# Last pair of the Mamba block: a new front with two convolution tiles on TensorE, the gate half later, and another order inside the loop over its states

## The chip, the cores and the metric

One core of one Trainium2 chip runs the whole program. It has five engines with a queue each: TensorE (PE) multiplies, VectorE (DVE), ScalarE (ACT) and GpSimd (POOL) work elementwise, and SyncE (SP) issues the DMAs. Each queue runs in its own order, and an instruction starts when the semaphores that it waits for have the counts asked for. The metric is the device time of one execution in microseconds, the median of the runs.

## The reference

```python
x = x + xattn(ctx, layernorm(x))          # 16 heads, 64 latents per sequence, 1024+64 keys
x = x + mamba(layernorm(x))               # below
x = x + ffn(layernorm(x))                 # 8 experts, each gathers tokens by a list and scatters back

# mamba, for x of (8, 64, 256): 512 inner channels, 16 states, 4 taps
xn = layernorm(x) * norm_w + norm_b
xc, z = split(xn @ W_in)
xc = silu(sum(x_pad[:, k:k + 64] * conv_w[:, k] for k in range(4)) + conv_b)
dbc = xc @ x_proj_w                       # 33 rows: one for dt, 16 of B, 16 of C
dt = softplus(dbc[0] * dt_w + dt_b)
h[n, t] = exp(dt * A[n]) * h[n, t-1] + dt * B[n, t] * xc      # for each of 16 states n
y = (sum_n h[n, t] * C[n, t] + xc * D) * silu(z)
out = y @ W_out + x
```

## The kernel before

**Stages.** The 8 sequences of 64 tokens form four pairs of 128 tokens (t = 0 to 3). The cross attention runs as 64 steps of a head pair, 8 for each sequence. The Mamba work of pairs 0 to 2 is woven into the attention steps: for each pair and state a unit `u = 16 t + n` is opened on POOL (`open_unit`, L630: work = dtx times B), scanned on DVE (`scan_unit`, L974), multiplied with C on POOL (`close_unit`, or late `times_c`, L752), and summed. For the last units TensorE adds the products up in PSUM bank `WB` (`sum_unit`, L1967). Eight units are left when the attention ends: u8, u9 and u10 of the drain, and `left[0]` to `left[4]`.

**The last pair (t = 3, INLINE)** can only start when the attention of its two sequences is done. Its front, one step behind the other: statistics and normalised tokens `xn`; two transposes to `xn_t`; `in_proj(0)` (the x half of W_in, four tiles of 128 channels) and `in_proj(1)` (the z half, the gate) on TensorE (L1795); four taps of the convolution over four tiles on DVE (L1163, L1166, 16 instructions); silu on ACT (`xc`, L1520); `x_proj` (L1802); `dbc` copied out (L1526); row 0 of `dbc` spread over the partitions by `spread` (L1813), from it the softplus on DVE and ACT (`dt_abs`, L1529 to L1531), then `dts_l` and `dtx_l` on DVE (L1194, L1197). Rows of B 0 to 3 come to `b_all` by TensorE and ACT (semaphore `m_b`), the others by three DMAs; rows of C come four at a time by `spread_out`.

**The loop over its 16 states**, in each engine's own order: POOL `drive` (L777, dtx_l times B, up to four ahead), ACT four exponentials into PSUM (L1558, bank `DB[n % 2]`), DVE the scan `state` (L1208) and `read` (L1218, state times C), TensorE adds `read` up in PSUM (`sum_states`, L2019, one matmul over 512 columns, which the trace shows as two records). Beside it the queues carry other work: the last units; `side_job` (transposes of `pick`, the one-hot token lists of the experts, L2024, and ACT's copy L1540, four states later; the transposed weights `coef_t`; two matmuls with b2); eight `slot_weight` (four matmuls each, L2062); `w_out` of pair 2 (L1808) and its residual; and the first `gather` matmuls.

**The way to the experts.** The normalised tokens of each pair are split in `f_hi` and `f_lo`. `gather(g, k, t)` is two matmuls over 512 columns (L2054) for expert group g, channel half k and pair t: 16 calls in all. Their four banks are copied to `xg_t` (L1577), then come W1 (L2147), Gelu (L1587, `hid`), W2 (L2157) and the way back to the tokens (L2134).

**What sets the order.** Every queue is written out by hand; there is no planner. Buffers: three `work` (a unit waits for the sum of the unit three before it), four `bc` rows loaded by DMA (each after the sum of the unit four before it), four `drive`, three `state`, two `read`. All of the last pair's queues are in the four blocks after `all_steps(body, drain)`.

## Time and profile before

| | us |
|---|---|
| median of 3 runs | 768.75 (768.65 to 770.01) |
| profiled execution, its time | 769.03 |
| its span, first to last instruction | 767.3 |
| PE, DVE, ACT, POOL busy in the span | 735.2, 493.9, 432.5, 399.7 |
| mean granted TensorE clock | 0.984 |

The attention's last matmul into the residual ends at 612.4 us and the first expert's second layer starts at 695.41 us; everything the change touches lies between these two times. "Busy" of PE counts pipelined matmuls with modelled ends, so it is read together with the granted clock and with the idle times in brackets, which name the engine and line that ended them.

### The profile page before, as it was taken

To read this page: it belongs to the slowest core of one execution; us is meant where nothing else is said; L and a number is where in the kernel's file an instruction comes from. 1 tells how busy PE (TensorE), PEld (TensorE's weight loads), DVE (VectorE), ACT (ScalarE), POOL (GpSimd) and SP (SyncE) were. 2 spreads that over 40 slices of the span, in tenths; PEclk is the share of its full clock that TensorE was granted. 3 is DMA by queue.
4 is the path that set the end of the run, shared out by engine and by line. 5 is a ranking of instruction groups with operands and counts; after the bars stand their busy time and mean duration, and the time that the engine had idled before them with its cause. 6 is when DMAs were issued, how large, how long until landed. Compare 5 with 4: busy or idle time off the path is not lost.

```text
span 767.3 us, 14591 instructions
## 1 busy us (share of the span) xinstructions
PE 735.2 (96%) x5539; PEld 681.3 (89%) x5539; DVE 493.9 (64%) x1061; ACT 432.5 (56%) x1135; POOL 399.7 (52%) x355
## 2 busy tenths in 40 slices
PE   8999999999999999999999999999999886999995
PEld 8889999999998999999989999999999663578885
DVE  7574574556574667858777778686798886840102
ACT  2546456546355766566578666666656553734331
POOL 6515315302610389658838986587397978730000
PEclk9999999999999999999999999999999995999999
DMA  8742100011001200310211022000100107703800
GB/s 308 243 138 60 63 25 2 1 62 25 2 5 59 53 16 1 95 34 16 65 32 34 15 68 55 15 15 1 33 15 21 28 22 234 254 1 129 285 26 30
DMA packets 51418, 49.62 MB, mean 65 GB/s; under 512 B 19524, under 2 KB 46352, under 8 KB 50320
## 3 DMA queue, kind: packets, MB, share of 16 engines
q1 hardware_dynamic: 51344, 48.64, 20.9%
q8 instruction: 46, 0.75, 0.4%
q14 instruction: 28, 0.23, 0.1%
HBM read 44.10 MB, written 4.52 MB: 63 GB/s over the span
## 4 chain that ended last, share of the span: by engine, by line
PE 69%; POOL 14%; issue 8%; DVE 5%; ACT 3%; DMA 1%; POOLq 0%; DVEq 0%
PE psum L1701 18%; PE psum L1736 17%; PE psum L1717 5%; PE psum L2157 4%; PE psum L2147 4%; POOL work L630 3%; PE psum L1670 3%; POOL work L637 2%; POOL y_sum L643 2%; PE psum L1767 2%; PE psum L1677 2%; PE psum L1795 2%; POOL drive L777 1%; PE psum L1611 1%; PE psum L1777 1%
## 5 line engine op out<-in xcount | busy, mean ns | idle before, releaser
L1347 ACT ACTIVATE pt_hi<-psum 128x512 fp32r<-128x512 f32 (+1 forms) x192 | 87.2, 489 | 179.9 <-PE psum L1717 122.0
L1736 PE MATMUL psum<-kvn_hi,pt_hi 128*128 128x256 f32 x512 | 150.1, 293 | 0.0
L1736 PE MATMUL psum<-kvn_hi,pt_lo 128*128 128x256 f32 x512 | 144.3, 282 | 0.0
L1736 PE MATMUL psum<-kvn_lo,pt_hi 128*128 128x256 f32 x512 | 144.2, 282 | 0.0
L1043 DVE TENSOR_REDUCE rowmax<-psum 128x1 f32<-128x728 f32 x64 | 58.6, 915 | 79.2 <-PE psum L1701 79.2
L1736 PEld LDWEIGHTS psum<-kvn_lo,pt_hi 128*128 128x128 f32 x512 | 97.4, 190 | 0.2
L1736 PEld LDWEIGHTS psum<-kvn_hi,pt_hi 128*128 128x128 f32 x512 | 97.1, 190 | 0.2
L1736 PEld LDWEIGHTS psum<-kvn_hi,pt_lo 128*128 128x128 f32 x512 | 97.1, 190 | 0.0
L1701 PE MATMUL psum<-kvt_hi,qk_hi 128*128 128x364 f32 (+1 forms) x384 | 90.5, 344 | 0.0
L896 DVE TENSOR_TENSOR pt_lo<-psum,pt_hi 128x512 fp32r<-128x512 f32 x128 | 82.0, 682 | 8.2 <-ACT pt_hi L1347 8.2
L637 POOL TENSOR_TENSOR work<-work,bc 128x512 f32<-128x512 f32 x40 | 54.3, 1357 | 58.6 <-DVE work L974 58.6
L1701 PE MATMUL psum<-kvt_hi,qk_lo 128*128 128x364 f32 (+1 forms) x384 | 84.5, 328 | 0.0
L1701 PE MATMUL psum<-kvt_lo,qk_hi 128*128 128x364 f32 (+1 forms) x384 | 84.5, 329 | 0.0
L974 DVE TENSOR_TENSOR_SCAN work<-dec,work 128x512 f32<-128x512 f32 x48 | 73.6, 1536 | 6.4 <-POOL work L630 6.1
L575 POOL TENSOR_SCALAR cvar<-cmv 128x8 f32<-128x8 f32 x8 | 1.9, 232 | 131.5 <-DVE cmv L835 131.1
L630 POOL TENSOR_TENSOR work<-dtx,bc 128x512 f32<-128x512 f32 x48 | 65.2, 1361 | 8.4 <-DMA bc<-dbc_keep 6.6
L1717 PE MATMUL psum<-ident,prob 128*128 128x128 f32 x512 | 66.5, 273 | 1.4 <-DVE pt_hi L893 0.8
L1701 PEld LDWEIGHTS psum<-kvt_lo,qk_hi 128*128 128x128 f32 x384 | 66.6, 188 | 0.0
L1701 PEld LDWEIGHTS psum<-kvt_hi,qk_lo 128*128 128x128 f32 x384 | 66.5, 188 | 0.0
L1701 PEld LDWEIGHTS psum<-kvt_hi,qk_hi 128*128 128x128 f32 x384 | 63.2, 189 | 2.2 <-issue 0.4
L1423 ACT ACTIVATE dec<-dts,a_neg 128x126 f32<-128x126 f32 x192 | 60.7, 394 | 5.9 <-DVE work L974 5.3
L1467 ACT ACTIVATE prob<-psum,nbias 128x728 f32<-128x728 f32 x64 | 55.7, 870 | 13.4 <-DVE nbias L1045 11.1
(251 smaller groups left out, 1576.5 us busy)
## 6 DMA issues: line engine op xcount, KB each, us to landing
w<-in_L_ffn_W_dram SPq DMA_DIRECT2D x16, 1024.0 KB, 8.2
ctx_nat<-in_ctx_dram SPq DMA_DIRECT2D x8, 1024.0 KB, 5.1
bc<-dbc_keep SPq DMA_DIRECT2D x48, 128.0 KB, 4.5
q_cur<-q_keep SPq DMA_DIRECT2D x14, 128.0 KB, 3.0
q_keep<-q_t SPq DMA_DIRECT2D x1, 1536.0 KB, 6.0
wq_sb<-in_L_xattn_Wq_dram SPq DMA_DIRECT2D x1, 1024.0 KB, 10.6
wk_nat<-in_L_xattn_Wkv_dram SPq DMA_DIRECT2D x1, 1024.0 KB, 12.7
wv<-in_L_xattn_Wkv_dram SPq DMA_DIRECT2D x1, 1024.0 KB, 14.7
```

The lines of the kernel that those rows point to most:

```text
L630: pool.tensor_tensor(work[u % WORKS][:], dtx[:], bc[u % ROWS][:, 0:1, :].to_broadcast((P, DT, P)), ALU.mult).then_inc(v_drv, 1)
L637: link(pool.tensor_tensor(work[u % WORKS][:], work[u % WORKS][:], bc[u % ROWS][:, 1:2, :].to_broadcast((P, DT, P)), ALU.mult))
L896: dve.tensor_tensor(pt_lo[u][:, t0:t1, :], where.rearrange("p (t m) -> p t m", m=P), pt_hi[u][:, t0:t1, :].bitcast(F32), ALU.subtract).the ...
L974: dve.tensor_tensor_scan(work[u % WORKS][:].rearrange(flat), dec[u % 2][:].rearrange(flat), work[u % WORKS][:].rearrange(flat), 0.0, ALU.m ...
L1043: dve.tensor_reduce(rowmax[slot][:, hp, 0:1], LG_A, XY, ALU.max)
L1347: act.activation(pt_hi[u][:, t0:t1, :], where[:, 0:(t1 - t0) * P].rearrange("p (t m) -> p t m", m=P), ACT.Copy)\
L1423: last = act.activation(seqs(dec[u % 2][:])[:, d, :, 1:], seqs(dts[:])[:, d, :, 1:], ACT.Exp, scale=a_neg[:, d, n:n + 1])
L1467: act.activation(prob[hp % 2][:, 0:2 * CUT].rearrange("p (a n) -> p a n", n=CUT), LG_A, ACT.Exp, bias=nbias[slot][:, hp:hp + 1], scale=SCA ...
L1701: last = pe.matmul(psum[:, n, 0:x1_ - x0], w, x_[slot][:, k, x0:x1_], start=first, stop=final)
L1717: last = pe.transpose(TP[n][:, j * P:(j + 1) * P], prob[hp % 2][:, (4 * n + j) * P:(4 * n + j + 1) * P], ident[:])
L1736: pe.matmul(PV, w[u][:, j, :], x_[slot][:, j, :], start=(j == 0 and w is pt_hi and x_ is kvn_hi), stop=False)
L2147: last = pe.matmul(psum[:, f % 4, 0:P], w1[i][:, k, f * P:(f + 1) * P], xg_t[:, k, RING * q + i, :], start=(k == 0), stop=(k == CK - 1))
```

## The change

It touches only the last pair, from the statistics to the first expert, and the places of other work in the same queues:

- **Convolution.** Tiles 2 and 3 (`PE_TILES`) leave DVE. ACT builds eight diagonal matrices `tap_w` (identity times one tap of a tile) after the drain; TensorE projects tiles 2 and 3 first, into bank `JB`; ACT copies them into the padded `xpad`; TensorE adds four products `tap_w` times shifted `xpad` for each tile; ACT's silu reads PSUM with the bias. DVE keeps 8 of its 16 tap instructions.
- **Gate half.** `in_proj(1)` moves behind the softplus input `v_dl`. ACT copies it and takes its silu after the loop.
- **Softplus.** Row 0 is spread twice; ACT takes Abs straight from PSUM with scale and bias, beside DVE's linear form.
- **Fillers.** The ten matmuls ahead of `x_proj` (`FILL_XC`) are gone.
- **Left units.** Of `left[0..4]`, DVE and POOL do two ahead of the loop in place of three, and three inside it (behind states 1, 3, 5 on DVE).
- **Slot weights and gathers.** The eight `slot_weight` move from states 12 to 15 to states 1 to 8, one for each; four gathers of pairs 0 and 1 sit behind states 12 and 13 in place of two calls at the end; `coef_slot` is reduced inside the loop.
- **Tokens for the experts.** POOL makes `f_hi` as well (ACT did), for pair 0 ahead of the loop, for pair 1 behind drive 11, for pair 2 behind the last drive. The last pair's `f_hi` comes from x directly on DVE.
- **Expert head.** The gathered banks are `GB = ((0, 1), (4, 7))`; ACT copies half k = 0 and DVE half k = 1. The Gelu table is loaded ahead of the gathers' end.
- `token_norm` of the last pair: the two small variance instructions go from POOL to DVE.

```diff
@@ POOL @@
-            for u in left[1:3]:
-                open_unit(u)
+            link(pool.memset(fhalf[:], -0.5))
...
+            open_unit(left[1])
             pool.wait_ge(r_pos, 2)
...
+            row_scale(0, 2)
+            pool.wait_ge(v_xt, INLINE + 2)
+            row_parts(0)
             times_c(left[0])
...
-            times_c(left[1])
-            open_unit(left[3])
-            times_c(left[2])
-            open_unit(left[4])
             pool.wait_ge(v_dtx, INLINE + 1)
             pool.wait_ge(m_b, 2)
-            for n in range(2):
+            drive_open(0)
+            drive_open(1)
+            open_unit(left[2])
+            drive_open(2)
+            times_c(left[1])
...
@@ DVE @@
-            scan_unit(left[0])
+            first_pick(1)
             dve.wait_ge(v_xz, INLINE + 1)
             dve.wait_ge(v_dts, INLINE)
+            own = DT - len(PE_TILES)
             for k in reversed(range(TAPS)):
                 late = TAPS - 1 - k
-                for d in range(DT):
+                for d in range(own):
...
@@ ACT @@
+                for k in range(TAPS):
+                    act.activation(tap_w[:, n, k, :], ident[:], ACT.Copy, scale=convw[:, d, k:k + 1])
...
+            act.wait_ge(m_xp, 1)
+            act.activation(xpad[:, PE_TILES[0]:, :, TAPS - 1:],
+                           psum[:, JB, 0:C].rearrange("p (d s l) -> p d s l", s=BP, l=L), ACT.Copy).then_inc(v_pad, 1)
...
+            for n, d in enumerate(PE_TILES):
+                act.wait_ge(m_cv, len(PE_TILES))
+                act.activation(xc[:, d, :], psum[:, JB, C + n * P:C + (n + 1) * P], ACT.Silu,
+                               bias=dvec[:, 0, d:d + 1]).then_inc(v_xc, 1)
...
+            act.wait_ge(m_dt0, 2)
+            for d in range(DT):
+                last = act.activation(dt_abs[:, d, :], psum[:, CB[1], 0:P], ACT.Abs, scale=dvec[:, 1, d:d + 1],
+                                      bias=dvec[:, 2, d:d + 1])
...
@@ PE @@
-            in_proj(0, psum[:, YB, :]).then_inc(v_xz, 1)
-            in_proj(1, psum[:, ZB, :]).then_inc(v_xz, 1)
+            in_proj(0, psum[:, JB, :], PE_TILES).then_inc(m_xp, 1)
+            in_proj(0, psum[:, YB, :], range(DT - len(PE_TILES))).then_inc(v_xz, 1)
...
-            sum_unit(u10)
-            fill(FILL_XC)
+            pe.wait_ge(v_pad, INLINE + 1)
+            for n, d in enumerate(PE_TILES):
+                for k in range(TAPS):
+                    last = pe.matmul(psum[:, JB, C + n * P:C + (n + 1) * P], tap_w[:, n, k, :], xpad[:, d, :, k:k + L],
+                                     start=(k == 0), stop=(k == TAPS - 1))
+                last.then_inc(m_cv, 1)
...
             pe.wait_ge(v_dl, INLINE + 1)
+            in_proj(1, psum[:, ZB, :]).then_inc(v_xz, 1)
+            sum_unit(u10)
...
-            sum_unit(left[1])
+            pe.wait_ge(m_dta, 1)
             spread_out(1)
-            sum_unit(left[2])
...
+                if 1 <= n <= E:
+                    last = slot_weight(n - 1)
+                    if n == E:
                         last.then_inc(f_cs, 1)
```

POOL's queue from the last `tshift` of the last pair to the first drives, before (work are the units' tiles, drive those of the loop):

```order
L656 TENSOR_SCALAR tshift<-tshift 128x1
L630 TENSOR_TENSOR work<-dtx,bc 128x512
L752 TENSOR_TENSOR work<-work,bc 128x512 x2
L630 TENSOR_TENSOR work<-dtx,bc 128x512 x2
L765 TENSOR_SCALAR coef_hl<-coef 128x32
L766 TENSOR_TENSOR coef_hl<-coef,coef_hl 128x32
L752 TENSOR_TENSOR work<-work,bc 128x512
L770 TENSOR_TENSOR y_skip<-xc,dvec 128x512
L752 TENSOR_TENSOR work<-work,bc 128x512
L630 TENSOR_TENSOR work<-dtx,bc 128x512
L752 TENSOR_TENSOR work<-work,bc 128x512
L630 TENSOR_TENSOR work<-dtx,bc 128x512
```

The first two drives come right behind these rows. The same stretch of POOL's queue after the change:

```order
L635 TENSOR_TENSOR work<-dtx,bc 128x512
L762 TENSOR_TENSOR work<-work,bc 128x512 x2
L772 MEMSET fhalf 128x4
L635 TENSOR_TENSOR work<-dtx,bc 128x512
L792 TENSOR_SCALAR coef_hl<-coef 128x32
L793 TENSOR_TENSOR coef_hl<-coef,coef_hl 128x32
L777 TENSOR_SCALAR fvar<-fmv 128x2
L778 TENSOR_TENSOR frstd<-fvar,fhalf 128x2
L782 TENSOR_SCALAR xn<-x,fmv,frstd 128x256
L785 TENSOR_SCALAR f_hi<-xn 128x256
L787 TENSOR_TENSOR f_lo<-xn,f_hi 128x256
L762 TENSOR_TENSOR work<-work,bc 128x512
```

Then come y_skip and the first two drives: two unit products and three unit openings have moved behind drives, and five instructions for the tokens of pair 0 have come in.

TensorE's queue behind the transposes of `xn` of the last pair, up to the spreads of `dbc`, before:

```order
L1795 MATMUL psum<-xn_t,win 128x128 x16
L1987 MATMUL psum<-ident,b_rows 128x64
L1967 MATMUL psum<-work,ident 128x512 x2
L1973 MATMUL psum<-ident 128x128 x10
L1802 MATMUL psum<-xc,wxp 33x128 x4
```

and after:

```order
L1859 MATMUL psum<-xn_t,win 128x128 x8
L2051 MATMUL psum<-ident,b_rows 128x64
L2031 MATMUL psum<-work,ident 128x512
L2056 MATMUL psum<-xpad,tap_w 128x128 x8
L1866 MATMUL psum<-xc,wxp 33x128 x4
L1877 MATMUL psum<-dbc,ident 128x128 x6
L1859 MATMUL psum<-xn_t,win 128x128 x8
```

Eight projections, one unit sum and the ten fillers have left the place ahead of `x_proj`, and eight tap matmuls stand there.

TensorE's queue inside the loop, from state 1 to state 3, after (read is summed by L2089, pick turned by L2094, the slot weights are L2132; before, the rows L2132 were absent here and stood, eight at a time, behind the sums of states 12 to 15):

```order
L2031 MATMUL psum<-work,ident 128x512
L2094 MATMUL psum<-ident,pick 128x128 x4
L2132 MATMUL psum<-coef_hl,pick 128x2 x4
L2089 MATMUL psum<-read,ident 128x512
L2094 MATMUL psum<-ident,pick 128x128 x4
L2132 MATMUL psum<-coef_hl,pick 128x2 x4
L2089 MATMUL psum<-read,ident 128x512
L2031 MATMUL psum<-work,ident 128x512
```

Each state from 1 to 8 now carries four small matmuls more, and every second one a unit's sum.

## Rows read from the trace of the kernel before

**Rows 1.** By stretch: length; busy PE, PEld, DVE, ACT, POOL; granted clock; DMA
```profile
627.00:640.50 13.50, 10.57 (x33) 5.85 (x34) 7.34 (x9) 8.59 (x26) 13.04 (x11) 0.63 0.15 43
640.50:647.00 6.50, 1.82 (x3) 0.25 (x1) 6.44 (x6) 2.47 (x8) 4.06 (x3) 0.50 1.00 302
647.00:651.00 4.00, 3.91 (x5) 1.85 (x6) 3.41 (x5) 1.24 (x4) 4.00 (x4) 0.50 1.06 390
651.00:667.00 16.00, 15.38 (x69) 9.15 (x69) 14.20 (x17) 11.94 (x35) 12.94 (x12) 1.00 0.95 331
667.00:680.80 13.80, 13.58 (x58) 7.30 (x56) 9.36 (x13) 7.54 (x22) 6.80 (x12) 1.00 0.00 1
```

**Rows 2.** Timeline of POOL: start, us, operation, idle before it and who ended it
```profile
617.04 1.27 POOL L630 TENSOR_TENSOR work<-dtx,bc 128x512 f32<-128x512 f32 x1
618.26 3.41 POOL L752 TENSOR_TENSOR work<-work,bc 128x512 f32<-128x512 f32 x2
622.98 1.27 POOL L630 TENSOR_TENSOR work<-dtx,bc 128x512 f32<-128x512 f32 x1 [1.30 <-PE psum L1967]
627.32 1.31 POOL L630 TENSOR_TENSOR work<-dtx,bc 128x512 f32<-128x512 f32 x1 [3.07 <-DMA bc<-dbc_keep]
...
639.19 2.48 POOL L777 TENSOR_TENSOR drive<-dtx_l,b_all 128x512 f32<-128x512 f32 x2
```

**Rows 3.** Groups by shape on POOL: count, busy us, mean ns, idle before
```profile
L803 POOL TENSOR_SCALAR dec<-x,fmv,frstd 128x256 f32<-128x256 f32 x3 | 3.7, 1227 | 0.7 <-POOL frstd L800 0.7
...
L806 POOL TENSOR_TENSOR f_lo<-dec,f_hi 128x256 fp32r<-128x256 f32 x3 | 2.2, 727 | 6.6 <-ACT f_hi L1595 6.6
```

**Rows 4.** Timeline of DVE, front, first state, last tokens
```profile
618.41 2.21 DVE L974 TENSOR_TENSOR_SCAN work<-dec,work 128x512 f32<-128x512 f32 x1 [0.89 <-POOL work L630]
...
621.80 3.13 DVE L1166 SCALAR_TENSOR_TENSOR conv<-psum,convw,conv 128x126 f32<-128x126 f32 x12
...
640.56 1.22 DVE L1208 TENSOR_TENSOR_SCAN state<-psum,drive 128x512 f32<-128x512 f32 x1 [5.00 <-POOL drive L777]
...
686.89 0.43 DVE L1253 TENSOR_TENSOR f_lo<-dec,f_hi 128x256 fp32r<-128x256 f32 x1 [0.49 <-ACT f_hi L1595]
```

**Rows 5.** Timeline of ACT, front of the last pair
```profile
625.29 1.28 ACT L1521 ACT_TABLE_LOAD   x1
...
626.95 0.27 ACT L1526 ACTIVATE dbc<-psum 33x128 f32<-33x128 f32 x1
...
630.52 0.63 ACT L1531 ACTIVATE dt_abs<-dt_abs 128x512 f32<-128x512 f32 x1
```

**Rows 6.** Timeline of PE, front and one state of the loop
```profile
617.73 3.84 PE L1795 MATMUL psum<-xn_t,win 128*128 128x128 f32 x32 [0.55 <-ACT xn_t L1511]
...
629.22 1.15 PE L1813 MATMUL psum<-dbc,ident 33*128 33x128 f32 x8 [0.57 <-DVE conv L1188]
...
652.97 1.02 PE L2019 MATMUL psum<-read,ident 128*128 128x512 f32 x2
653.83 0.60 PE L2024 MATMUL psum<-ident,pick 128*128 128x128 f32 x4
654.27 1.02 PE L2019 MATMUL psum<-read,ident 128*128 128x512 f32 x2
```

**Rows 7.** Chain that ended last, in order of time: start, us, what
```profile
678.56 0.79 PE psum L2062 x8
...
682.12 1.73 PE psum L1808 x8
683.85 5.14 PE psum L2054 x22
...
689.01 2.07 ACT xg_t L1577 x4
...
691.09 1.28 ACT L1582
...
695.41 3.72 PE psum L2157 x16
```

230 lines of the change are left out of this document (136 added, 94 removed).

## The prediction

> **What bounds the kernel now.** I read the busy times by stretch first, then the timelines of the engines that wait, then the chain. Three regimes follow one another. From 627 to 640.5 POOL is busy 13.04 of 13.50 us while DVE has 7.34 [rows 1]: POOL's queue of unit products and openings holds back the first drive, which starts at 639.19 [rows 2], and DVE's first state scan waits 5.00 us for it, to 640.56 [rows 4]. Up to 651 the queue of DVE and POOL goes on. TensorE has 1.82 of 6.50 us between 640.5 and 647, at a granted clock of 0.50 (1.2 GHz). From 651 on the clock is full and TensorE is busy 15.38 of 16.00 and 13.58 of 13.80 us [rows 1]: it bounds the rest of the loop, and in the chain its rows follow one another without a gap to w_out at 682.12 [rows 7]. The third regime is the way to the first second layer at 695.41: gathers, then 2.07 us of copies and 1.28 us of table load on ACT, both bare in the chain [rows 7]. Time won in the front is therefore worth only what TensorE's own list after 645 leaves of it, and time won in the third regime counts in full.
>
> **Front.** DVE's taps lose half of their instructions: the 12 with an addition took 3.13 us [rows 4], six take about 1.6. The x half is 16 matmuls in two halves; the two halves together with the gate were 3.84 us at 617.73, 0.24 a matmul (32 records, two to a matmul) [rows 6]. So tiles 2 and 3 are projected after 0.96 us and tiles 0 and 1 after 1.92, at 619.7, about as late as before for DVE, which then ends at 622. The eight tap matmuls cost 8 x 0.24 = 1.9 us. They stand behind the sum of u9, whose product POOL ends about 620.8 (1.27 + 2 x 1.2 to 1.7 us from 617.04 [rows 2]), so they run from 621.7 to 623.6, and silu ends near 624.3. Before, the table load behind silu began at 625.29 [rows 5]; it now begins about 1.0 us earlier. The row of dbc comes at 625.9 in place of 626.95. The diagonal matrices are ACT work while ACT waits for the norm, priced at nothing. If that cover were gone they would cost 8 instructions of some 0.3 us, since four silus of the same shape at about 0.25 ended just ahead of 625.29. The ten fillers stood where TensorE waited for silu anyway: nothing.
>
> Behind dbc the softplus needs Abs, Exp and Ln. The last took 0.63 [rows 5]; Abs in four pieces is between 0.63 and 1.3, I take 1.0. It starts from the second spread, without DVE's linear form between them. dts_l and dtx_l are then there at 630.5 to 631. The other input of a drive is b_all, which now lies behind the gate half (8 x 0.24 = 1.9), the sum of u10 (0.9) and four spreads (1.15 at 629.22, eight records [rows 6]) from v_dl at 627.8: 631.7, and ACT's copy makes it 632.3.
>
> **POOL** decides, as before. Its queue from 617.04 to the first drive: two openings and four products (6 x 1.27 = 7.6), y_skip 1.27, coef_hl 1.6, and for pair 0 the scale 0.8, the normalised rows 1.23, f_hi and f_lo. f_lo took 0.73 [rows 3]; f_hi on POOL has no row, between 0.4 and 1.23, and I take 0.5, since it reads one operand where f_lo reads two. Sum 13.7, less one product counted in the 620.8 (left[1]'s now lies behind drive 2), 12.4. Collisions come on top: the two products at 618.26 took 3.41 beside DVE's scan of 2.21 [rows 2, 4], against 2 x 1.27 and a free scan's 1.22, so about 0.9 each time. Four such meetings are 3.6. First drive at 617.04 + 12.4 + 3.6 = 633.0, and the first scan at about 635.3, some 5.2 us earlier than 640.56. What vanishes is 1.30 us of waiting for a sum and 3.07 us for a row's DMA [rows 2], and two products and three openings that went behind drives.
>
> **Loop.** Those units now sit between drives 1 and 8. POOL (some 14 items at 1.24 to 1.7 us each up to drive 8) and DVE (three unit scans) therefore keep the first states slow, and state 0's lead shrinks already there. The sum of state 1 starts near 644.5. From there TensorE's list to the last sum is: 15 state sums and 4 unit sums at 0.86 (652.97 to 653.83) to 0.98, I take 0.89, 16.9; eight turnings at 0.44 (653.83 to 654.27) 3.5 [rows 6]; eight slot weights at 0.79 for two [rows 7] 3.2; two spreads of four 2.2; w_out 1.73; four gather calls at 2 x 5.14/22 = 0.47 [rows 7] 1.9; coef_t 0.44, b2 two at 0.89, 1.8. Together 31.7 us. At half clock the sums double; before, the clock was back at full by 651 [rows 1]. I take 650, three sums at half, 2.6 us. The last sum ends at 644.5 + 31.7 + 2.6 = 678.8, the gate product and its two semaphores add 0.9 to 1.0, so w_out starts at **679.8** against 682.12: 2.3 us of the front's 5.2. The rest is given back because TensorE, once full, was the bound already, and slot weights and gathers that move to the front of its list don't become less. The waits ahead of the slot weights (f_hl, m_b) were met long before. The wait ahead of the first gathers is for the second b2 copy, and behind it the sum of state 13 and DVE's last reads are queued; the copy takes some 0.6 beside a sum of 0.89, so it costs 0 to 0.3, taken as 0 since the copy was asked for a state earlier. The zs silu now comes after the exponentials, with a table load of 1.28 [rows 5]: the last exponentials end near 675.5, so it is done about 677.9, one microsecond ahead of need. If the loop came out faster than I say, this would be late next.
>
> **Head of the experts.** Before, 695.41 - 682.12 = 13.3 us [rows 7]. Now: w_out 1.73; 12 gather calls (14 before, behind w_out) at 0.47, 5.6; the first layers of two experts, 16 matmuls at 0.24, 3.8; the last Gelu 0.4 with its semaphores. 11.6 us, **1.7** less: two calls, and ACT's copies and table load no longer in the path, since group 0 is copied by ACT and DVE while group 1 is gathered. The cover of the last pair's normalisation shrinks from ten calls to eight, 3.7 us; before, f_lo came at 687.3, 3.5 us after w_out ended [rows 4, 7]. DVE's own f_hi takes out ACT's round trip, so it keeps inside. If not, it costs a few tenths.
>
> The trace has a table load of 1.28 us with the next ACT instruction 0.01 us behind it [rows 5, 7]. The Trainium skill, page ScalarE: Activation LUTs, section What ACT_TABLE_LOAD costs, puts a drain of about 1.38 us on top, 2.66 in all. By it the head would give 3.1 and the sum 763.3; the row speaks against it.
>
> **Sum.** 2.3 + 1.7 = 4.0 off the profiled 769.03, 765.0; the median of the runs lies 0.3 below the profiled run, so **764.7**. About 0.2% (1.5 us) is what a measurement can tell from no change.
>
> **Rivals.** *B, POOL jams.* Five token instructions and two openings stand ahead of drive 0 beside DVE's picks and scans. If every one collides as at 618.26, the first drive is 2.2 us later, 635.2, and nearly all of it reaches w_out: 766.7. For: 3.41 and 2.21 [rows 2, 4]; against: the reads of the taps come from PSUM. The Trainium skill, page SBUF — State Buffer, section 🔬 SBUF: two separate sides, makes it an exclusive lock: a GpSimd instruction and a DVE instruction with two SBUF inputs never share, the later one waits whole. These rows fit it.
>
> *C, the clock is back early.* With less idle time for TensorE than before its clock may not fall, or return by 647. Of the 2.6 us above about 1.2 come back, then DVE and POOL bound: 763.5.
>
> *D, the clock falls early.* The fillers and two sums leave the place ahead of x_proj. If TensorE is at 0.5 from 627 (before, the mean was 0.63 over 627 to 640.5 [rows 1]), gate half, sum and spreads take 3.9 more, the first drive waits for b_all until about 636, and some half of that is swallowed later: 766.3.
>
> *E, the front doesn't come.* Silu's products on TensorE wait for ACT's copy of the projections and for the sum of u9. If x_proj is no earlier and POOL's drives come one microsecond earlier only, sum 1 is at 648.5, w_out at 682, and the head's 1.7 us alone is left, less the loss of a wait at state 12: 767.7.
>
> *A, slower.* TensorE's list is now heavier in states 1 to 8. If the clock stays at 0.5 beyond 650, each microsecond costs about 0.4 (half of the time is sums and spreads that double). The gain is gone when full clock comes at 660; at 664.5 the time is 4.0 - 0.4 x 14.5 = -1.8: 770.5. Against it: at 651 the clock rose with a busy TensorE for four microseconds [rows 1].
>
> **Chances.** Forecast (763.8 to 765.9) 0.50; B 0.12; C 0.12; D 0.10; E 0.10; A 0.06. Faster by over 0.2%: 0.50 + 0.12 + 0.12 + 0.10 = 0.84; within 0.2% E, 0.10; slower A, 0.06. The range leaves out E and A and the tail of C: 762.8 to 767.5. It covers f_hi's bounds (0.1 less, 0.7 more) and the wait at state 12 (0.3).
>
> **What would show it.** In the timeline of POOL the first drive at 632.5 to 634 (B: over 635, with products of 2 us and more); in ACT's, dbc at 625.9 (E: 626.5 or later); in the stretches, the clock at full by 650 and TensorE busy 96% from there to 678; state 15 scanned near 674.5, w_out at 679.8, the second layer at 691.4. I am wrong on the loop if w_out is over 681 while the first scan is at 635.5 and the clock as said; wrong on the head if w_out to the second layer is over 12.3 us.

## The result and the profile after

| | before | changed |
|---|---|---|
| median, us | 769.04 (768.65 to 770.01, 5 runs) | 764.62 (763.97 to 765.90, 5 runs) |
| ratio | | 0.9943, 95% interval 0.9932 to 0.9955 |
| profiled execution: time, span | 769.03, 767.3 | 764.62, 762.8 |

Three differences between the two profiled spans make up the 4.5 us, read from the timelines of PE. From the start to the last pair's w_out: 681.96 before, 678.55 after, 3.41 less (0.40 of it was there when the attention ended, 612.42 and 612.02, which the change doesn't touch). From w_out to the first second layer: 13.45 before, 11.76 after, 1.69 less. From there to the end of the span: 71.89 before, 72.49 after, 0.60 more.

By stretch, the changed kernel (length; busy PE, PEld, DVE, ACT, POOL; granted clock; DMA share; GB/s), to set beside [rows 1]:

```profile
622.00:626.00 4.00, 2.77 (x24) 2.31 (x23) 3.27 (x5) 2.45 (x5) 3.64 (x6) 1.00 0.14 35
626.00:630.00 4.00, 3.66 (x20) 3.46 (x19) 2.25 (x5) 3.65 (x10) 3.83 (x5) 0.57 0.00 0
630.00:634.00 4.00, 4.00 (x22) 2.36 (x21) 2.54 (x2) 2.18 (x7) 1.73 (x2) 1.00 0.09 18
...
642.00:645.00 3.00, 1.91 (x3) 0.88 (x4) 2.17 (x3) 3.00 (x11) 2.81 (x3) 0.50 0.92 301
645.00:648.00 3.00, 3.00 (x12) 1.77 (x11) 3.00 (x4) 0.53 (x2) 3.00 (x3) 0.67 1.04 370
648.00:651.00 3.00, 3.00 (x14) 1.74 (x13) 2.85 (x5) 2.91 (x10) 3.00 (x4) 1.00 1.05 395
651.00:667.00 16.00, 16.00 (x87) 11.33 (x86) 13.53 (x17) 10.32 (x30) 15.83 (x14) 1.00 0.94 328
```

TensorE is busy without a gap from 645 to the last state's sum at 677.8, and the clock is full again at about 647.0, 4 us earlier than before the change (651). From 626 to 630 the granted clock was 0.57 although TensorE was busy 3.66 of 4.00 us. PE's timeline has the gate half in that stretch, and later the first sums, which wait for DVE's reads:

```profile
626.93 3.48 PE L1859 MATMUL psum<-xn_t,win 128*128 128x128 f32 x16 [0.34 <-DVE conv L1224]
...
639.68 2.07 PE L2089 MATMUL psum<-read,ident 128*128 128x512 f32 x2 [4.14 <-DVE read L1253]
643.09 2.07 PE L2089 MATMUL psum<-read,ident 128*128 128x512 f32 x2 [1.33 <-DVE read L1253]
644.96 1.92 PE L2031 MATMUL psum<-work,ident 128*128 128x512 f32 x2
```

The gate half (8 matmuls, 16 records) took 3.48 us; before the change it was half of the 3.84 us in [rows 6]. POOL's timeline, to set beside [rows 2]:

```profile
617.47 3.48 POOL L762 TENSOR_TENSOR work<-work,bc 128x512 f32<-128x512 f32 x2
...
629.37 1.48 POOL L800 TENSOR_TENSOR y_skip<-xc,dvec 128x512 f32<-128x512 f32 x1
633.12 2.48 POOL L807 TENSOR_TENSOR drive<-dtx_l,b_all 128x512 f32<-128x512 f32 x2 [2.27 <-ACT b_all L1596]
```

POOL's queue was through at 630.85; it then waited 2.27 us for ACT's copy of the B rows. The first scan on DVE answers to [rows 4]:

```profile
634.49 1.22 DVE L1243 TENSOR_TENSOR_SCAN state<-psum,drive 128x512 f32<-128x512 f32 x1 [1.95 <-POOL drive L807]
```

So the first scan came 6.07 us earlier (640.56 to 634.49). From it to the sum of state 2, 13.15 us where it had been 12.41 (652.97 less 640.56): 0.74 given back. From that sum to w_out, 30.91 where it had been 28.99: 1.92 given back. The second number is TensorE's list. Behind the sum of state 2 stand three unit sums more than before (3 x 0.86 = 2.6) and two gather calls more (0.9), and the slot weights take 0.8 less (7 x 0.34 in place of 8 x 0.40): 2.7 together. PE's busy time in this stretch grew by 2.0 only, from 28.15 to 30.13 us, and its idle time hardly changed (0.84 before; 0.78 after, which is all the wait for the gate product ahead of w_out). The other 0.7 us are my reading, not a measurement: before the change a sum twice started 0.75 us behind a turning (659.64 to 660.39, 661.35 to 662.10) where turnings otherwise take 0.44, because it waited for DVE's read, and the modelled ends count that wait as busy.

This also corrects a reading in the prediction. Before the change, the chain was not TensorE's alone from 651 on. It ran over POOL's drives and DVE up to 662, and over TensorE mainly from there:

```profile
649.97 7.38 POOL drive L777 x6
...
661.38 0.67 DVE read L1218
...
671.61 1.13 PE psum L2019 x2
```

TensorE, POOL and DVE were close to level in that loop; only with the change does TensorE run it without a gap.

**What moved the first drive.** Before the change its two inputs were there at 633.35 (dtx_l) and 631.64 (b_all), and POOL's queue reached it at 639.19. After it they are there at 631.40 and 632.99, and the queue is through at 630.85. By these times nearly all of the 6.07 us is the unit work that went behind the drives, with its waits of 1.30 and 3.07 us [rows 2]: without it the old front's inputs would have let the drive start at about 633.4. The rest of the front had to keep up with it. No run put that work back, so this is read from two timelines and not shown by an experiment.

The chain of waits of the changed kernel at the end of the loop and in the head, beside [rows 7]:

```profile
677.81 0.70 DVE dtx_l L1279
...
678.55 1.99 PE psum L1872 x8
680.55 5.62 PE psum L2124 x24
686.17 3.70 PE psum L2220 x32
...
689.89 0.38 ACT hid L1651
...
690.31 3.72 PE psum L2232 x16
```

ACT's copies and its table load are gone from the chain. The load for Gelu now lies at 675.86, and the zs silu ends at 675.84, 2 us ahead of the gate product that reads it (677.81):

```profile
673.92 1.28 ACT L1657 ACT_TABLE_LOAD   x1
675.21 0.63 ACT L1657 ACTIVATE zs_l<-zs_l 128x512 f32<-128x512 f32 x1
675.86 1.28 ACT L1658 ACT_TABLE_LOAD   x1
```

### The profile page after: what moved, and what is told of

It reads as the page before. It is cut to its first block, busy times and chain, and to the rows that moved or that the text cites. A ratio compares the mean times of both kernels' runs of the same rounds, so it can differ in the third digit from the quotient of the medians.

```text
span 762.8 us, 14589 instructions
## 1 busy us (share of the span) xinstructions
PE 732.2 (96%) x5537; PEld 681.2 (89%) x5537; DVE 497.9 (65%) x1058; ACT 435.8 (57%) x1142; POOL 397.7 (52%) x354
## 4 chain that ended last, share of the span: by engine, by line
PE 73%; POOL 11%; issue 6%; DVE 6%; ACT 3%; POOLq 0%; DVEq 0%; ACTq 0%
PE psum L1765 18%; PE psum L1800 17%; PE psum L1781 5%; PE psum L2220 4%; PE psum L2232 4%; PE psum L1734 3%; POOL work L635 3%; PE psum L2089 2%; POOL work L642 2%; POOL y_sum L648 2%; PE psum L1831 2%; PE psum L1741 2%; PE psum L1859 1%; PE psum L1815 1%; PE psum L1675 1%
## 5 line engine op out<-in xcount | busy, mean ns | idle before, releaser
L1009 DVE TENSOR_TENSOR_SCAN work<-dec,work 128x512 f32<-128x512 f32 x48 | 75.4, 1575 | 5.1 <-POOL work L635 4.9
```

Source lines behind the costliest of these rows:

```text
L1009: dve.tensor_tensor_scan(work[u % WORKS][:].rearrange(flat), dec[u % 2][:].rearrange(flat), work[u % WORKS][:].rearrange(flat), 0.0, ALU.m ...
```

## The experiments

Every experiment starts from the changed kernel. Each was run five times or more beside the kernel before; the ratio is to that. For the timelines, one execution of each was profiled, and the table at the end has them side by side.

### Does POOL's queue set the first drive?

```diff
+            link(pool.tensor_tensor(y_skip[:], xc[:], dvec[:, 3, :].unsqueeze(2).to_broadcast((P, DT, P)), ALU.mult))
             pool.tensor_tensor(y_skip[:], xc[:], dvec[:, 3, :].unsqueeze(2).to_broadcast((P, DT, P)), ALU.mult)\
```

> The changed kernel with one more POOL product of 1.27 us (y_skip written twice) ahead of the first drive; the result is the same. In the changed kernel POOL's queue waits 2.27 us for ACT's copy b_all before the first drive at 633.12. Theory b_all (TensorE's gate half, unit sum and spreads set the first drive): the extra product lies in that wait, the first drive stays at 633.1, the time at 764.6 within 0.4. Theory POOL (the prediction's, POOL's own queue sets it): the first drive comes 1.3 later, 634.4, and the time is 765.3 to 765.9.

Measured: 764.61 (764.25 to 766.21), ratio 0.9944 (0.9931 to 0.9957), the changed kernel's. POOL's timeline:

```profile
630.72 1.37 POOL L801 TENSOR_TENSOR y_skip<-xc,dvec 128x512 f32<-128x512 f32 x1
634.36 2.49 POOL L808 TENSOR_TENSOR drive<-dtx_l,b_all 128x512 f32<-128x512 f32 x2 [2.27 <-ACT b_all L1597]
```

The first drive of this execution is 1.2 us later, but not because of the added product. It ends at 632.1, and POOL still waits 2.27 us for b_all. The granted clock was 0.50 from 626 to 630 and 0.65 from 630 to 634, so that the gate half and the sum behind it took 3.78 and 1.91 us. The wait for b_all sets the drive, and TensorE's clock sets b_all.

### The gate half back in front

```diff
             in_proj(0, psum[:, YB, :], range(DT - len(PE_TILES))).then_inc(v_xz, 1)
+            in_proj(1, psum[:, ZB, :]).then_inc(v_xz, 1)
...
             pe.wait_ge(v_dl, INLINE + 1)
-            in_proj(1, psum[:, ZB, :]).then_inc(v_xz, 1)
```

> The gate half of the projection goes back to TensorE's place right behind the x half; all else as changed. Theory b_all: the eight matmuls end at 620.9 in place of the unit sum starting at 619.8, so the taps, silu, dbc and dtx_l come 1.0 later (dtx_l ready at 632.4 in place of 631.4), but 3.48 us of half-clock work leave the path of b_all, which is then early; first drive 632.4 to 632.6, 0.6 earlier than 633.12, time 764.0 to 764.4. Rival (moving the gate half shortened the front): first drive 634.1, 1.0 later, time 765.3 to 765.6.

Measured: 764.22 (763.90 to 766.35), ratio 0.9948 (0.9935 to 0.9960). The first drive started at 631.92 and met DVE, so that two drives took 3.40 us and the first scan was at 634.2. The time is what the theory of b_all gives, and the front's rival, 765.3 and more, falls. In this execution the clock fell too, but later, to 0.81 from 628 to 630 and 0.50 behind it, long after the gate half; b_all was there at 631.57, and dtx_l (631.84) set the first drive. Moving the gate half out of the front brought nothing that can be measured here: what it takes out ahead of x_proj it puts ahead of b_all.

### The convolution tiles back on DVE

```diff
-            in_proj(0, psum[:, JB, :], PE_TILES).then_inc(m_xp, 1)
-            in_proj(0, psum[:, YB, :], range(DT - len(PE_TILES))).then_inc(v_xz, 1)
+            in_proj(0, psum[:, YB, :]).then_inc(v_xz, 1)
...
-                    last = pe.matmul(psum[:, JB, C + n * P:C + (n + 1) * P], tap_w[:, n, k, :], xpad[:, d, :, k:k + L],
-                                     start=(k == 0), stop=(k == TAPS - 1))
...
-            own = DT - len(PE_TILES)
+            own = DT
```

> All four convolution tiles on DVE again, no diagonal matrices, no tap matmuls; all else as changed. Both theories: 8 more tap instructions at 0.27 make silu's end about 2.0 later (625.3 in place of 623.3) and the first drive 635.1 in place of 633.1. Theory list (TensorE's list from the sum of state 1 is as long as it is, so what shifts its start shifts its end): w_out about 1.8 to 2.0 later, time 766.4 to 766.7. Theory given back (about half of any change in the front is lost in the loop, as 3.0 of 5.7 us came through): time 765.4 to 765.7.

Measured: 766.96 (765.30 to 767.61, 8 runs), ratio 0.9970 (0.9960 to 0.9981). The first drive was at 635.61 and w_out at 681.24, 2.5 and 2.7 us later than with the change: what shifts the start shifts the end, and nothing of it is given back. Theory "given back" falls. But the 2.0 us that I had put down to eight DVE instructions were something else. PE's timeline of this kernel:

```profile
624.13 1.92 PE L1856 MATMUL psum<-xc,wxp 128*33 128x128 f32 x8 [3.03 <-ACT xc L1570]
...
626.40 2.92 PE L1867 MATMUL psum<-dbc,ident 33*128 33x128 f32 x12 [0.36 <-ACT dbc L1574]
629.26 3.63 PE L1849 MATMUL psum<-xn_t,win 128*128 128x128 f32 x16
```

x_proj starts 0.7 us later only (623.40 with the change). It then takes 1.92 us where it took 1.06, and the six spreads 2.92 where they took 1.60. TensorE had waited 3.03 us for silu; the granted clock was 0.59 from 622 to 624 and 0.50 from there to 632. So of the 2.5 us at the first drive, 0.7 are the convolution and some 1.8 came while the clock was at half. That the tap matmuls hold the clock up by standing where the ten fillers had stood is argued from this one execution: no kernel had the taps on DVE and the fillers back.

### The expert head as before

```diff
-                    for k in range(1 if isinstance(r, int) else CK):
+                    for k in range(CK):
...
             act.activation(zs_l[:], zs_l[:], ACT.Silu).then_inc(m_zs, 1)
-            act.activation(warm_out[:], a_neg[:, 0, 0:1], ACT.Gelu_apprx_tanh)
...
-                        dve.tensor_copy(xg_t[:, 1, g * RING:(g + 1) * RING, :],
-                                        psum[:, GB[g][1], :].rearrange("p (e s) -> p e s", s=P)).then_inc(f_gatd, 1)
```

> The expert head as before: ACT copies all four gathered banks and loads the Gelu table behind them; gathers, banks and all else as changed. Theory (copies and table load were in the path): W2 starts 1.28 for the load and about 0.6 for two copies later, 692.1 in place of 690.3, time 766.2 to 766.6. Rival (the two gather calls fewer are the whole gain of the head, ACT's work was beside TensorE's): 764.6 to 765.0.

Measured: 765.76 (763.34 to 767.33), ratio 0.9961 (0.9946 to 0.9975). The six runs lie 4 us apart, so the median, which falls between the two forecasts, says little here. In the profiled execution w_out to the second layer was 12.64 us where it is 11.76 with the change: 0.88, half of what I expected. The other 0.81 of the head's 1.69 is near the two gather calls fewer (0.94). The chain of this kernel in the head shows why it is not 1.28 plus two copies:

```profile
683.75 2.06 ACT xg_t L1635 x4
...
685.83 1.28 ACT L1641
...
687.64 2.07 PE psum L2213 x16
```

TensorE works on the first layer of expert 0 while the table is loaded, so the path holds one first layer of 2.07 us, where with the change it holds both in a row, 3.70. This execution also shows the front with an undisturbed clock: 1.00 from 626 to 634, the first drive at 631.51, w_out at 677.51, 1.0 us earlier than in the changed kernel's execution, with the same instructions up to there but for ACT's Gelu load, which nothing waited for.

### The changed kernel once more

> The changed kernel, unedited, once more, beside the next three. Theory clock (in some executions the granted clock falls to half during the gate half and the spreads, 626 to 631, in others it doesn't, and this alone moves the first drive between 631.5 and 634.4): the runs scatter by about 2 us, median 764.2 to 765.0, and where this execution's clock is 1.00 from 626 to 631 its first drive is at 631.5, where it is 0.5 there the drive is at 633.1 or later. Rival (the first drive is set by queues alone): 633.1 whatever the clock.

Measured: 764.47 (763.88 to 764.61), ratio 0.9935 (0.9921 to 0.9948). Clock 0.63 from 626 to 630, first drive 633.52, behind b_all again. With the undisturbed execution above (631.51) and the one with the longest stretch at half clock (634.36), the rival, a drive at 633.1 whatever the clock, falls. The scatter was smaller than the 2 us that I had expected.

### The rows of B ahead of the gate half

```diff
             pe.wait_ge(v_dl, INLINE + 1)
-            in_proj(1, psum[:, ZB, :]).then_inc(v_xz, 1)
-            sum_unit(u10)
             for j in range(4):
                 last = spread(psum[:, DTB, j * P:(j + 1) * P], 1 + j)
             last.then_inc(m_b, 1)
+            in_proj(1, psum[:, ZB, :]).then_inc(v_xz, 1)
+            sum_unit(u10)
...
-            act.wait_ge(v_xz, INLINE + 2)
-            act.activation(zs_l[:], psum[:, ZB, :].rearrange("p (d m) -> p d m", m=P), ACT.Copy).then_inc(m_zs, 1)
             act.wait_ge(m_b, 1)
             act.activation(b_all[:, 0:4, :], psum[:, DTB, :].rearrange("p (n m) -> p n m", m=P), ACT.Copy)\
                 .then_inc(m_b, 1)
+            act.wait_ge(v_xz, INLINE + 2)
+            act.activation(zs_l[:], psum[:, ZB, :].rearrange("p (d m) -> p d m", m=P), ACT.Copy).then_inc(m_zs, 1)
```

> The four spreads of B come ahead of the gate half and the unit sum on TensorE, and ACT copies b_all ahead of the gate half. Theory b_all: b_all is there by 630.5 at either clock, the first drive is then set by dtx_l (631.4) at 631.5, 1.6 earlier than 633.12, the loop of 44.0 us from the first scan to w_out is as long as before, time 763.0 to 763.4. Rival (POOL's queue or the collisions behind it set the first scan): first drive no earlier than 632.5, time 764.2 to 764.8.

Measured: 764.02 (763.26 to 764.40), ratio 0.9930 (0.9917 to 0.9944). That lies between what the two theories had said. b_all was copied by 630.0 and the first drive started at 631.30, as expected, and the first scan at 634.67 all the same. POOL's timeline:

```profile
631.30 3.40 POOL L807 TENSOR_TENSOR drive<-dtx_l,b_all 128x512 f32<-128x512 f32 x2 [0.63 <-DVE dtx_l L1232]
...
644.66 1.27 POOL L807 TENSOR_TENSOR drive<-dtx_l,b_all 128x512 f32<-128x512 f32 x1 [1.91 <-DMA b_all<-dbc_keep]
```

and DVE's:

```profile
634.67 1.22 DVE L1243 TENSOR_TENSOR_SCAN state<-psum,drive 128x512 f32<-128x512 f32 x1 [2.32 <-ACT psum L1621]
```

Two new waits took the place of the old one. The scan waited for ACT's exponentials, which stand behind ACT's copy of the gate half. And drive 4 waited for the DMA of the other B rows, of which more below.

### Fewer slot weights

```diff
-                if 1 <= n <= E:
+                if n == 1:
                     last = slot_weight(n - 1)
-                    if n == E:
-                        last.then_inc(f_cs, 1)
+                if n == E:
+                    last = slot_weight(n - 1)
+                    last.then_inc(f_cs, 1)
```

This kernel leaves out six of the eight slot weights, so its result is not that of the reference.

> Six of the eight slot weights are left out (the experts' weights are then wrong), so TensorE's list has 24 small matmuls less between states 2 and 7. Theory list (TensorE bounds the loop from the sum of state 1): each was 0.34 us in the chain of waits, first scan to w_out 42.0 in place of 44.0, time 762.6 to 763.0. Rival (DVE, ACT and POOL are as close: POOL has 15.83 of 16.00 us from 651 to 667): less than 0.7 comes out, 764.0 to 764.6.

Measured: 764.28 (762.23 to 764.98), ratio 0.9929 (0.9916 to 0.9943). By the median the rival wins, by the trace neither. The sum of state 13 starts at 670.94, 1.5 us earlier than in the changed kernel's second execution (672.50), with the sum of state 2 at the same time in both (648.05 and 648.09). So 1.5 of the 2.0 us left out came through, and TensorE's list did get shorter. Then the clock fell. Windows of this kernel:

```profile
670.00:672.00 2.00, 2.00 (x5) 0.77 (x5) 1.88 (x3) 1.61 (x6) 1.83 (x3) 0.83 0.00 0
672.00:674.00 2.00, 2.00 (x5) 1.23 (x4) 1.69 (x3) 1.98 (x4) 0.03 (x1) 0.50 0.01 4
674.00:676.00 2.00, 2.00 (x6) 1.17 (x6) 0.98 (x3) 1.97 (x3) 0.00 (x0) 0.81 0.00 0
```

TensorE is busy throughout, and from the sum of state 13 to w_out it is 7.97 us where it is 6.48: the fall cost 1.5, and w_out comes at 678.91, as if nothing had been left out. The one run at 762.23 is what the list theory had forecast; that the fall was absent in it is my reading, since its trace wasn't taken.

### The slot weights where TensorE is idle

```diff
+                if n == 0:
+                    pe.wait_ge(f_hl, 1)
+                    pe.wait_ge(m_b, 2)
+                    pe.wait_ge(f_pick, 1)
+                    for e in range(E // 2):
+                        slot_weight(e)
+                if n == 1:
+                    for e in range(E // 2, E):
+                        last = slot_weight(e)
+                    last.then_inc(f_cs, 1)
                 sum_states(n)
...
-                if n == 1:
-                    pe.wait_ge(f_hl, 1)
-                    pe.wait_ge(m_b, 2)
-                if 1 <= n <= E:
-                    last = slot_weight(n - 1)
-                    if n == E:
-                        last.then_inc(f_cs, 1)
```

> The eight slot weights go to where TensorE is idle: four ahead of the sum of state 0 and four ahead of the sum of state 1, in place of one behind each of states 1 to 8. Theory list: TensorE waited 4.14 us ahead of the sum of state 0 and 1.33 ahead of that of state 1, so they cost at most 0.5 there and take 2.4 to 2.7 out of the list; first scan to w_out 41.5 to 42.2, time 762.2 to 763.0. Rival (at half clock they push the sum of state 1, or the work only changes places because POOL and DVE hold the loop): 764.0 to 764.8.

Measured: 766.86 (766.02 to 768.38, 7 runs), ratio 0.9974 (0.9963 to 0.9985): slower than the changed kernel by 2.4 us (764.47 in its second measurement), and slower than either theory had said. PE's timeline:

```profile
637.98 3.55 PE L2132 MATMUL psum<-coef_hl,pick 128*128 128x2 f32 x16 [2.52 <-DVE pick L1068]
641.39 2.05 PE L2089 MATMUL psum<-read,ident 128*128 128x512 f32 x2
642.46 4.19 PE L2132 MATMUL psum<-coef_hl,pick 128*128 128x2 f32 x16
646.51 2.05 PE L2089 MATMUL psum<-read,ident 128*128 128x512 f32 x2
```

The first sixteen could not start in the wait for the reads as I had meant: their inputs include DVE's last pick, which ended at 637.84 only. Sixteen of these matmuls took 3.55 and 3.20 us in the chain (the row of 4.19 above overlaps the sum ahead of it), 0.20 to 0.22 each, where four took 0.34 in the changed kernel's chain at full clock. The clock was 0.50 in every stretch from 638 to 651, four microseconds longer than in the changed kernel, though TensorE was busy in all of them. The sum of state 1 came 3.4 us later. From the sum of state 2 to w_out it was 29.6 where it is 30.9, so the list did shrink, by less than was paid for.

### Fillers in the front

```diff
+            fill(2)
             sum_unit(u9)
...
+            fill(3)
             pe.wait_ge(v_xc, INLINE + DT)
...
+            fill(2)
             pe.wait_ge(v_dbs, INLINE + 1)
```

> Seven fillers (128 columns each, as the ten that the change took out) in TensorE's waits of the front: two ahead of the sum of u9, three ahead of x_proj, two ahead of the first spreads. Theory clock (the idle time in the front lets the granted clock fall in the gate half): the clock stays at 1.00 from 626 to 630, the gate half takes about 2.0 in place of 3.5 us, b_all is copied by 631.4, first drive 631.5 as it was in the execution with the old expert head, time 762.8 to 763.6. Rival (the fall at 626 doesn't hang on these waits): clock 0.5 to 0.7 there again, first drive 633.1 or later, time 764.2 to 764.9.

Measured: 763.37 (763.01 to 765.92), ratio 0.9925 (0.9912 to 0.9938). Windows of this kernel, from 622 to 630:

```profile
622.00:626.00 4.00, 3.95 (x33) 3.44 (x31) 3.21 (x6) 2.79 (x6) 3.64 (x5) 1.00 0.15 30
626.00:630.00 4.00, 3.66 (x26) 2.71 (x25) 2.25 (x4) 3.80 (x10) 3.83 (x5) 1.00 0.00 0
```

and its first drive in POOL's timeline:

```profile
631.36 3.15 POOL L807 TENSOR_TENSOR drive<-dtx_l,b_all 128x512 f32<-128x512 f32 x2 [0.88 <-ACT b_all L1596]
```

The clock stayed at 1.00 through the gate half and b_all came by 631.22. One execution of the old-head kernel had that without fillers, so it is one observation for the theory, not proof, and the last kernel below speaks against it. Three of its five runs lie at 763.0 to 763.4. Its profiled execution, 765.92, had the good front and then a fall of the clock at 672 to 676 that cost it 1.5 us (from the sum of state 13 to w_out 7.94 us in place of 6.48).

### Fillers in the loop

```diff
+                if n < 2:
+                    for _ in range((15, 7)[n]):
+                        pe.matmul(psum[:, JB, 0:P], ident[:], ident[:], start=True, stop=True)
                 sum_states(n)
```

> Fillers where TensorE waits for the first two reads: 15 ahead of the sum of state 0 and 7 ahead of that of state 1 (3.6 and 1.7 us at full clock). Theory clock (the wait of 4.1 us ahead of the first sum brings the clock to half until 646.5, and the two state sums, the unit sum and the first turning pay about 2.3 us for it): clock 1.00 from 630 on, sum of state 2 at 646.0 or earlier in place of 647.6, first scan to w_out 42.3 to 43.0, time 762.8 to 763.6. Rival (DVE and POOL hold states 2 to 5, so faster sums come to nothing): w_out within 0.4 of the changed kernel's, time 764.2 to 764.9; if the clock falls all the same the fillers take twice as long and the time is over 765.

Measured: 764.49 (762.19 to 769.01, 12 runs), ratio 0.9946 (0.9928 to 0.9964). The clock was 1.00 from 630 to 648, as the clock theory says, and the sum of state 2 started at 645.49 in place of 647.64. The next one then waited:

```profile
649.09 1.18 PE L2089 MATMUL psum<-read,ident 128*128 128x512 f32 x2 [1.70 <-DVE read L1253]
650.06 1.91 PE L2031 MATMUL psum<-work,ident 128*128 128x512 f32 x2
```

The median is the rival's, and in the profiled execution both theories are half right: the sums were faster, DVE and POOL then held the next read, and the clock fell behind the new wait (0.52 and 0.50 from 650 to 653), so w_out came at 679.82. The runs spread from 762.2 to 769.0, wider than any other kernel's.

### The start of the first scan, and all of it together

On top of the rows of B ahead of the gate half:

```diff
             last.then_inc(v_dl, 1)
+            first_pick(2)
             dve.wait_ge(m_dta, 1)
...
-            first_pick(2)
...
-            act.wait_ge(v_xz, INLINE + 2)
-            act.activation(zs_l[:], psum[:, ZB, :].rearrange("p (d m) -> p d m", m=P), ACT.Copy).then_inc(m_zs, 1)
...
             for n in range(NS):
+                if n == 1:
+                    act.wait_ge(v_xz, INLINE + 2)
+                    act.activation(zs_l[:], psum[:, ZB, :].rearrange("p (d m) -> p d m", m=P), ACT.Copy).then_inc(m_zs, 1)
...
```

> As b_first (spreads of B ahead of the gate half), and what held its first scan mended: ACT makes the exponentials of state 0 ahead of its copy of the gate half, and DVE's third pick moves from behind dtx_l, where it met drive 0, into DVE's wait for the softplus. Theory list (what shifts the first scan shifts w_out, 44 us behind it): first drive 631.3 to 632.0, first scan 632.6 to 633.3 in place of 634.5, w_out 676.6 to 677.4, time 762.9 to 763.6. Rival (an earlier start is given back because the clock falls earlier as well and the loop gets longer, as b_first's 43.5 and the other executions' 43.6 to 44.8 differ): time 764.0 to 764.6.

Measured: 764.18 (762.34 to 764.41), ratio 0.9926 (0.9913 to 0.9938). By the median the rival wins. The first drive was at 632.57 and the scan at 633.9, since the pick met POOL. DVE's timeline has the pick:

```profile
627.19 1.22 DVE L1068 TENSOR_TENSOR pick<-iota_f,slot_of 128x1024 fp32r<-128x1024 f32 x1
```

and POOL's timeline the instruction that it met, and drive 4:

```profile
627.36 1.31 POOL L785 TENSOR_SCALAR f_hi<-xn 128x256 fp32r<-128x256 f32 x1
...
645.76 1.56 POOL L807 TENSOR_TENSOR drive<-dtx_l,b_all 128x512 f32<-128x512 f32 x1 [2.68 <-DMA b_all<-dbc_keep]
```

f_hi took 0.40 us in the changed kernel and 1.31 here: it ended at 628.67, 0.26 us behind the end of the pick (628.41). The Trainium skill, page SBUF — State Buffer, section 🔬 SBUF: two separate sides, calls this an exclusive lock for the whole instruction. This row agrees with it, since f_hi ended only once the pick had. Drive 4 waited 2.68 us for its rows. Their loads are the last of SP's queue, behind the row of a unit that waits for a unit's sum on TensorE: SP stored dbc at 636.2 though ACT had it at 625.3.

The last kernel has both, the fillers of the front (its TensorE edits are those shown above), the picks elsewhere and another order on SP:

```diff
-            for u in units_at[AFTER][3:]:
-                load_rows(u)
-            sp.wait_ge(r_cnt, 1)
-            sp.dma_start(b2_sb[:], b2).then_inc(ld_b2, 16)
             sp.wait_ge(v_acc, NS * (INLINE - 1))
             sp.wait_ge(v_dbs, INLINE + 1)
...
                 sp.dma_start(b_all[:, 4 * q:4 * q + 4, :], part.to_broadcast((P, 4, P))).then_inc(ld_ball, 16)
+            for u in units_at[AFTER][3:]:
+                load_rows(u)
+            sp.wait_ge(r_cnt, 1)
+            sp.dma_start(b2_sb[:], b2).then_inc(ld_b2, 16)
...
-            first_pick(2)
...
                 if n == 0:
-                    first_pick(3)
+                    first_pick(2)
...
                     read_open(n - 1)
+                if n == 1:
+                    first_pick(3)
```

> Everything that the executions so far pointed to: the seven fillers of the front; spreads and copy of B ahead of the gate half; ACT's exponentials of state 0 ahead of its copy of the gate half; DVE's two last picks behind scans 0 and 1; and on SP the store of dbc and the three loads of b_all ahead of the last two rows of the units, which wait for a unit's sum on TensorE (these three DMAs were issued at 637.9 in the changed kernel, though dbc was ready at 624.9, and in b_first and b_first2 drive 4 waited 1.9 and 2.7 us for them). Theory list with the DMA gate gone: drive 0 at 631.2 to 631.6, scan 0 at 632.5 to 632.9 (634.5 in the changed kernel), no wait for a DMA at drive 4, scan 0 to w_out 44 us, w_out 676.4 to 677.2, time 762.2 to 763.0. Rival (POOL and DVE, which share the picks, drives, openings and scans of states 0 to 5, hold the sum of state 2, and the earlier scan 0 is lost by then): w_out 677.8 or later, time 763.4 to 764.2.

Measured: 764.76 (764.40 to 767.23, 6 runs), ratio 0.9953 (0.9940 to 0.9966). The first drive came at 631.15, the first scan at 632.52, 2.0 us earlier than in the changed kernel, and no drive waited for a DMA. The rival was right: w_out was at 679.25, and the time is 0.5 us above even its range. DVE's timeline:

```profile
632.52 1.22 DVE L1241 TENSOR_TENSOR_SCAN state<-psum,drive 128x512 f32<-128x512 f32 x1 [1.45 <-POOL drive L807]
633.66 2.29 DVE L1068 TENSOR_TENSOR pick<-iota_f,slot_of 128x1024 fp32r<-128x1024 f32 x1
...
637.58 1.79 DVE L1068 TENSOR_TENSOR pick<-iota_f,slot_of 128x1024 fp32r<-128x1024 f32 x1
639.30 2.28 DVE L1009 TENSOR_TENSOR_SCAN work<-dec,work 128x512 f32<-128x512 f32 x1
641.50 1.19 DVE L1241 TENSOR_TENSOR_SCAN state<-psum,drive 128x512 f32<-128x512 f32 x1
```

The two picks, taken out ahead of the first scan, stand behind it and meet POOL there; the scan of state 2 is at 641.5 in place of 641.3, and nothing of the 2.0 us is left. The sum of state 2 is even 0.8 us later (648.4 for 647.6), with the clock at 0.50 up to 648. The place of the second pick was mine, so this shows that picks, drives, openings and scans up to state 2 don't become less by another order; it doesn't show that no order is better.

PE's timeline of this kernel bears on the fillers:

```profile
627.73 3.65 PE L1861 MATMUL psum<-xn_t,win 128*128 128x128 f32 x16
```

TensorE was busy 3.96 of 4.00 us from 622 to 626, with the same seven fillers, and the clock fell all the same, to 0.50 from 628 to 630. So idle time ahead of x_proj is not what decides alone whether the clock falls in the gate half.

### The executions side by side

| kernel | clock 626 to 630 | first drive | first scan | sum of state 2 | w_out | scan to sum 2 | sum 2 to w_out |
|---|---|---|---|---|---|---|---|
| before | 1.00 | 639.2 | 640.6 | 653.0 | 682.0 | 12.4 | 29.0 |
| changed | 0.57 | 633.1 | 634.5 | 647.6 | 678.6 | 13.1 | 30.9 |
| changed, again | 0.63 | 633.5 | 634.9 | 648.1 | 679.0 | 13.2 | 30.9 |
| extra POOL product | 0.50 | 634.4 | 635.7 | 649.5 | 680.5 | 13.8 | 31.0 |
| gate half in front | 0.91 | 631.9 | 634.2 | 647.1 | 678.0 | 12.9 | 30.9 |
| taps on DVE | 0.50 | 635.6 | 637.0 | 650.2 | 681.2 | 13.2 | 31.0 |
| old head | 1.00 | 631.5 | 633.6 | 646.7 | 677.5 | 13.1 | 30.8 |
| fillers in front | 1.00 | 631.4 | 633.4 | 647.1 | 679.8 | 13.7 | 32.7 |
| fillers in loop | 0.57 | 632.9 | 634.2 | 645.5 | 679.8 | 11.3 | 34.3 |
| rows of B first | 0.50 | 631.3 | 634.7 | 646.8 | 678.2 | 12.1 | 31.4 |
| the same, scan mended | 0.63 | 632.6 | 633.9 | 647.6 | 678.7 | 13.7 | 31.0 |
| all together | 0.74 | 631.2 | 632.5 | 648.4 | 679.3 | 15.9 | 30.9 |

The last column is the list: 30.8 to 31.0 us in eight executions whose first scans lie 4.5 us apart, 31.4 in one, and more only where the clock fell inside it. (The two kernels with fewer or earlier slot weights have another list and are left out of the table.) That the list bounds the loop is also what leaving out slot weights showed, up to the fall of the clock: 1.5 of 2.0 us. No version clearly beats the changed kernel. Fillers in the front have the lowest median, 763.37, but their interval (0.9912 to 0.9938) overlaps that of the changed kernel (0.9921 to 0.9948 in its second measurement).

## Why the prediction was right, and where its steps were not

**The time.** 764.7 was forecast, 764.62 measured. The mechanism held in the large: a front several microseconds shorter, about half of it lost to TensorE's list, and the head's gain in full. The hit to 0.1 us is luck. Against the 765.0 that the sum gives for the profiled execution, w_out came 1.25 us early (0.40 of it before the change begins), the head was 0.16 longer, the end 0.60 longer, and the time exceeds the span by 0.1 more. And the 0.3 that I took off for the median was not there: the kernel before measured 769.04 in this comparison, as its profiled execution (769.03).

**The taps and the norm.** DVE's six taps took 1.61 us (1.6 said), dbc came at 624.66 (625.9 said). Of the 1.2 us, 0.7 was there at the transposes of xn already: 616.05 where it had been 616.75, 0.40 from the attention's end and 0.30 from the two variance instructions on DVE, which I had left out of the sum. What I got wrong in kind is what the taps on TensorE are worth, which the experiment with the taps on DVE shows: mostly the clock, in that execution. (My "16 matmuls" of the x half are 16 records, 8 matmuls; the prices worked out from them are right.)

**POOL decides.** This step failed. I priced four collisions at 0.9 us each; the queue ran from 616.25 to 630.85, 14.6 us where I had 16.0, and the added product then showed that 1.27 us more in it cost nothing. The first drive was at 633.12 where I had 633.0, but because b_all was late, so the agreement is luck: it started 0.9 us earlier than I had reckoned and then lost 1.6 in the gate half at half clock. That was rival D's event, at the place named, in an execution that otherwise ran as forecast; it cost 1.6 us there, which is the difference to the 631.5 of undisturbed fronts, and 1.0 at w_out, where I had put 3.9 and about half. The prediction's numbers for the two inputs of the drive (dtx_l 630.5 to 631, b_all 632.3; measured 631.40 and 632.99) were nearer to what decided than its text. The next step was off too: I put 2.3 us between first drive and first scan (633.0 to 635.3), where the rows before have 1.37 (639.19 to 640.56) and the changed kernel has 1.37 again. That is 0.8 us of the first scan's coming earlier than I said.

**The loop.** Sum of state 1 at 643.1 (644.5 said), full clock by about 647.0 (650 said), last sum's end at 677.8 (678.8 said), w_out at 678.55 (679.8 said). The list of 31.7 us at full clock and 2.6 for half clock was forecast as 34.3 and measured as 34.7 (643.1 to 677.8), which again is a cancellation. The 15 state sums took 0.98 us each where I had 0.89 (1.3 more) and the two b2 0.3 more; half clock cost about 2.0 in place of 2.6, and the slot weights 0.5 less (0.34 one by one, 0.79 for two). And before the change the chain from 650 to 662 ran over POOL and DVE, not over TensorE, as shown above: that the loop was TensorE's alone from 651 on was misread. Rival A's event, half clock deep into the loop, did come in single executions, but at 671 to 676 and for 1.5 us, not at 650 to 660.

**The head.** 11.6 said, 11.76 measured. The row that I read against the drain was right: behind the load at 673.92 the silu starts at 675.21, 0.01 us after its end, so the 2.66 us for a switch, as the Trainium skill, page ScalarE: Activation LUTs, section What ACT_TABLE_LOAD costs, has it, is not what these rows show. Had it been, my sum would have given 763.3.

**What was not in the sum.** The end, from the first second layer to the last instruction, was 0.6 us longer. Up to the last gathers back to the tokens nothing changed (63.40 us before, 63.39 after). From DVE's last addition to `acc_t` to the first of the final transposes it was 0.87 before and 1.34 after, where the profile shows no engine at work, and the transposes themselves ran at a clock of 0.50 (758 to 760), where before it was 0.90 (762 to 764). Over the kernels of this study the end took 71.7 to 72.6 us; I can't say that the change moves it.

**Rivals.** B (POOL jams) didn't come: POOL met DVE ahead of the first drive (two products 3.48 us, coef_hl 1.02, fvar 0.98), but was through at 630.85, and the drives that took 2.2 us stood behind it. C (the clock back early) was so in part: the clock was back at 647.0, which is worth 0.6 us of the list. D's event came, and A's in single executions, both smaller than priced. E (the front doesn't come) was wrong.
